# A GRU recurrence on one core: the new state from two VectorE scans, and one product group per step fewer

## The chip, the cores and the metric

The kernel runs on one core of a Trainium2 chip. The figure of merit is the device time of one execution in microseconds. A core has a matrix engine (TensorE, PE in the rows; PEld is its weight load), VectorE (DVE), ScalarE (ACT), GpSimd (POOL) and SyncE (SP, here only the queue that issues DMAs). They run side by side and wait for one another on semaphores.

## The reference

Two layers with residuals. The first is a mixture of four experts and one shared branch (each a GELU feed-forward 256 -> 1024 -> 256), which touches every row of `x` by itself. The second is a GRU over the 1024 rows of each of two sequences:

```python
def step(h, xs):
    xzt, xrt, xht = xs
    z = jax.nn.sigmoid(xzt + h @ U_z + vz)
    r = jax.nn.sigmoid(xrt + h @ U_r + vr)
    hh = jnp.tanh(xht + r * h @ U + vh)
    h_new = (1.0 - z) * h + z * hh
    return (h_new, h_new)
```

`h` has 256 features for each of 2 sequences. The 1024 steps depend on one another; the input products (`xz`, `xr`, `xh`) do not. `r * h @ U` is `(r * h) @ U`.

## The kernel before, in words

Time is cut into 8 chunks of 128 steps, a chunk into 8 bodies of 16 steps. The state lies with its features on the 128 partitions: 2 halves (`KC`) by 2 sequences (`B`), so 4 numbers per partition (`ST`). A sigmoid is written as a tanh of half its argument.

`U` in fp32 would be slow, so each of the three gate matrices is split into fp16 parts `u_high` and `u_mid`; the moving side is split too, into a HI and a LO fp16 part. The LO part is scaled up by 1024 or 2048 to stay inside fp16, and multiplies `u_low`, a third copy of `u_high` that is scaled down by the same factor. One "group" of a gate and a moving quantity is then 12 small products (`recur`, line 931): 8 with HI (`u_high`, `u_mid`; 2 output halves by 2 input halves) and 4 with LO. Each has 40 moving columns (`FILL`), of which 2 carry data and 38 are zeros. The sums collect in PSUM (`r_ps`, `z_ps`, `c_ps`) on top of the input part that `inject` (line 923) puts there once per body.

The `r` gate of the next step is not fed with the new state. The state is `h = A + Q`, with `A` the old state times (1 - z) and `Q` = z times the candidate. `A` is known before the candidate, so `old_state` (line 967) multiplies it early, and after the candidate's tanh only `Q` is multiplied. This is two groups for `r`, one for `z` (the whole new state, parts H_HI and H_LO) and one for the candidate (parts P_HI and P_LO, from `r * h`): 48 products per step.

Each engine has its own program, written out by hand. One step `t` on TensorE (`gru_body`, line 974): `r` with Q, `z` with H, window 0 of other work, candidate `c` with P, window 1 of other work, `r` of the next step with A. The other work (`gap_work`, line 944) is the feed-forward layer of the next chunk in fp32, cut into "units" (`FFN_UNITS`): every window has one unit, window 1 has two at t = 4 to 10, 12 and 14. The last body of a chunk also holds the input products of the next chunk (`gate_input`). The last chunk (steps 896 to 1023) has no feed-forward work left.

ScalarE runs the three tanhs (`gate_tanh`, line 480: r, z, c), GELUs and copies. VectorE (`gru_body`, line 687) runs 18 operations on 4 elements a step: lines 704 to 707 make P after the tanh of `r`; lines 712 to 721 make A after the tanh of `z`; lines 726 to 743 make Q, H and what the next step needs after the tanh of `c`. GpSimd splits the input parts of each body into bf16 (lines 337 to 353), scales the experts' hidden tiles (line 256) and adds the residual (`add_body`, line 355). Two bodies form one turn of a hardware loop; at the end of a turn each engine branches back.

Of the kernel before, what the change touches and what calls it, by code (L numbers as in the profile page):

```python
# [23 lines left out]
ALU = mybir.AluOpType  # L24
# [7 lines left out]
P = 128  # L32
# [3 lines left out]
LOW = 1024.0  # L36
PLOW = 2048.0
# [9 lines left out]
def moe_gru_kernel(nc, x, cond, gate_w, gate_b, time_w, time_b, ew1, eb1, ew2, eb2, sw1, sb1, sw2, sb2,  # L47
# [54 lines left out]
    with ctx:  # L102
# [29 lines left out]
        u_low = sb("u_low", [P, GATES, KC, D], F16)  # L132
# [4 lines left out]
        h_body = sb("h_body", [P, KC, SC])  # L137
# [12 lines left out]
        h_scale = sb("h_scale", [P, 1])  # L150
# [17 lines left out]
        parts = sb("parts", [P, 8, KC, FILL], F16)  # L168
        P_HI, P_LO, A_HI, A_LO, Q_HI, Q_LO, H_HI, H_LO = range(8)
        tanh_out = sb("tanh_out", [P, GATES, ST])  # L170
        st = sb("st", [P, 9, ST])
        PP, V, VV, A, AA, ZZ, QQ, HK, HH = range(9)
# [6 lines left out]
        rows_ps = xp_ps[1]  # L179
        gate_v = [g[:, 0:KC * SC].rearrange("p (m s b) -> p m s b", m=KC, b=B) for g in gate_ps]  # L180
# [63 lines left out]
        PARTS_STEP, STATE_STEP = 8, 9  # L244
# [72 lines left out]
        def _(pool):  # L317
# [37 lines left out]
            def add_body(c, j):  # L355
# [3 lines left out]
                pool.tensor_scalar(h_true[:, :, :], h_body[:, :, :], w_scale[:, :], None, ALU.mult  # L359
                                   ).then_inc(h_unscaled, 1)  # L360
                wait_apart(h_unscaled, n + 2)
# [29 lines left out]
            for g in range(GATES):  # L391
                pool.tensor_scalar(u_low[:, g, :, :], u_high[:, g, :, :],
                                   1.0 / (PLOW if g == C else LOW), None, ALU.mult).then_inc(u_split, 1)

            pool.wait_ge(scales_made, 1)
            pool.wait_ge(gate_scales_made, 2)
            split(0, 0)
            with pool.Fori(0, CH - 2) as c:
                with pool.Fori(0, BODIES - 1) as j:
                    split(c, j + 1)  # L400
                    scale_tiles(c + 1, j + 1)
                    add_body(c, j)
                scale_tiles(c + 2, 0)
                split(c + 1, 0)
                add_body(c, BODIES - 1)
            with pool.Fori(0, BODIES - 1) as j:
                split(CH - 2, j + 1)
                scale_tiles(CH - 1, j + 1)
                add_body(CH - 2, j)
            split(CH - 1, 0)  # L410
            add_body(CH - 2, BODIES - 1)
            with pool.Fori(0, BODIES - 1) as j:
                split(CH - 1, j + 1)
                add_body(CH - 1, j)
            add_body(CH - 1, BODIES - 1)


        @block.scalar
# [665 lines left out]
```

## Time and profile before

| | us |
|---|---|
| median of three runs | 2524.52 (2524.43 to 2530.35) |
| span of the profiled execution | 2531.0 |
| TensorE busy | 2338.1 (92%) |
| VectorE busy | 2022.5 (80%) |
| ScalarE busy | 755.4 (30%) |
| GpSimd busy | 337.8 (13%) |

The profiled execution's own time is its span, 2531.0 us; the profile lists nothing around it. That is 6.5 us over the median of the runs. TensorE's busy time counts a product from the moment it enters to its modelled end (about 180 ns), while the next one follows after about 25 ns, so a busy share near one does not say that the engine has no room. It is better to measure a step from the tanh rows on ScalarE: each gate has one per step, and they are never hidden by others.

### The profile page before, as it was taken

Reading aid. Unit: us, or ns where it says so; the run is one execution under the profiler, and the core shown is the slowest. Engines: PE = TensorE matmul, PEld = TensorE weight load, DVE = VectorE, ACT = ScalarE, POOL = GpSimd, SP = SyncE. Lnnn points to the kernel's source line nnn. Section 1 sums busy time; section 2 is a strip of 40 time slices with the busy share of each in tenths; the row PEclk is TensorE's granted clock in tenths of the full one; section 3 lists DMA queues with packets and bytes.
Section 4 is the critical chain, followed back from the end, with each engine's and each line's share of the span. In section 5 each row is a group of like instructions: output and inputs, shape, how many; then the busy total and the mean of one; then the engine's idle time right before and its main releaser. Section 6 shows DMA issues by size and latency. Waiting matters only on the chain.

```text
span 2531.0 us, 141144 instructions
## 1 busy us (share of the span) xinstructions
PE 2338.1 (92%) x54923; PEld 2166.7 (86%) x54923; DVE 2022.5 (80%) x18594; ACT 755.4 (30%) x3670; POOL 337.8 (13%) x623
## 2 busy tenths in 40 slices
PE   7999999999999999999999999999999898998888
PEld 5798898888988899888998889888898898977777
DVE  5288887888878888788878888788888887888888
ACT  2332233332332333322333233332233232232222
POOL 3011111111111111111111111111111111100000
PEclk8999999999999999999999999999999999998899
DMA  4411111111111111111111111111111111000000
GB/s 144 124 47 38 44 39 34 45 35 38 44 35 38 45 37 40 37 38 38 44 37 36 44 37 42 40 35 38 44 40 33 45 37 36 24 5 5 4 5 5
DMA packets 143677, 99.88 MB, mean 39 GB/s; under 512 B 13664, under 2 KB 142999, under 8 KB 143004
## 3 DMA queue, kind: packets, MB, share of 16 engines
q1 hardware_dynamic: 141840, 90.49, 12.5%
q8 instruction: 465, 7.62, 1.3%
q14 instruction: 208, 1.70, 0.2%
q10 hardware_dynamic: 1164, 0.07, 0.0%
HBM read 88.41 MB, written 2.10 MB: 36 GB/s over the span
## 4 chain that ended last, share of the span: by engine, by line
PE 73%; DVE 18%; issue 6%; ACT 2%; DMA 0%; DVEq 0%; SPq 0%; POOL 0%; POOLq 0%; ACTq 0%
PE r_ps L936 25%; PE up_ps L878 13%; PE c_ps L936 12%; PE y_ps L896 12%; PE z_ps L936 8%; DVE parts L704 2%; DVE parts L707 2%; ACT tanh_out L482 2%; PE xp_ps L910 2%; DVE st L714 1%; DVE st L743 1%; DVE parts L729 1%; DVE st L705 1%; DVE st L712 1%; DVE parts L741 1%
## 5 line engine op out<-in xcount | busy, mean ns | idle before, releaser
L936 PE MATMUL r_ps<-parts,u_high 128*128 128x40 f16 x8192 | 671.9, 182 | 108.4 <-issue 90.2
L936 PE MATMUL r_ps<-parts,u_mid 128*128 128x40 f16 x8192 | 664.0, 180 | 0.0
L936 PEld LDWEIGHTS r_ps<-parts,u_high 128*128 128x128 f16 x8192 | 543.4, 97 | 140.1 <-issue 91.8
L878 PE MATMUL up_ps<-feat,up_w 128*128 (+2 forms) x2380 | 542.1, 322 | 0.0
L936 PE MATMUL r_ps<-parts,u_low 128*128 128x40 f16 x8192 | 536.6, 182 | 3.5 <-DVE parts L729 2.3
L936 PEld LDWEIGHTS r_ps<-parts,u_mid 128*128 128x128 f16 x8192 | 516.3, 97 | 13.0 <-issue 1.1
L896 PE MATMUL y_ps<-hidden,down_w 128*128 128x128 f32 (+1 forms) x2380 | 496.9, 314 | 8.3 <-DVE hidden L256 8.3
L704 DVE SCALAR_TENSOR_TENSOR parts<-tanh_out,st 128x4 f16<-128x4 f32 x1024 | 197.4, 193 | 322.7 <-ACT tanh_out L482 258.9
L482 ACT ACTIVATE tanh_out<-r_ps 128x4 f32<-128x4 f32 x1024 | 177.2, 173 | 870.1 <-PE r_ps L936 870.1
L936 PE MATMUL c_ps<-parts,u_high 128*128 128x40 f16 x4096 | 349.9, 183 | 33.8 <-DVE parts L704 12.5
L878 PEld LDWEIGHTS up_ps<-feat,up_w 128*128 128x128 f32 x2380 | 367.4, 196 | 9.5 <-issue 3.0
L896 PEld LDWEIGHTS y_ps<-hidden,down_w 128*128 128x128 f32 x2380 | 345.9, 192 | 19.4 <-DVE hidden L256 12.2
L482 ACT ACTIVATE tanh_out<-c_ps 128x4 f32<-128x4 f32 x1024 | 177.5, 173 | 611.7 <-PE c_ps L936 611.7
L936 PEld LDWEIGHTS r_ps<-parts,u_low 128*128 128x128 f16 x8192 | 350.1, 97 | 10.2 <-DVE parts L729 3.6
L936 PEld LDWEIGHTS c_ps<-parts,u_high 128*128 128x128 f16 x4096 | 263.2, 97 | 109.5 <-DVE parts L704 53.8
L936 PE MATMUL z_ps<-parts,u_high 128*128 128x40 f16 x4096 | 343.1, 181 | 0.0
L936 PE MATMUL z_ps<-parts,u_mid 128*128 128x40 f16 x4096 | 342.2, 181 | 0.0
L936 PE MATMUL c_ps<-parts,u_mid 128*128 128x40 f16 x4096 | 340.8, 180 | 0.0
L936 PE MATMUL c_ps<-parts,u_low 128*128 128x40 f16 x4096 | 272.0, 182 | 9.5 <-DVE parts L707 6.9
L936 PE MATMUL z_ps<-parts,u_low 128*128 128x40 f16 x4096 | 268.8, 182 | 10.9 <-DVE parts L741 10.5
L936 PEld LDWEIGHTS c_ps<-parts,u_mid 128*128 128x128 f16 x4096 | 259.5, 97 | 7.4
L936 PEld LDWEIGHTS z_ps<-parts,u_mid 128*128 128x128 f16 x4096 | 257.7, 97 | 0.0
(137 smaller groups left out, 4577.5 us busy)
## 6 DMA issues: line engine op xcount, KB each, us to landing
up_w<-in_L_cond_ew SPq DMA_DIRECT2D x256, 128.0 KB, 2.4
down_w<-in_L_cond_ew SPq DMA_DIRECT2D x256, 128.0 KB, 2.1
up_w<-in_L_cond_sw SPq DMA_DIRECT2D x64, 128.0 KB, 3.0
down_w<-in_L_cond_sw SPq DMA_DIRECT2D x64, 128.0 KB, 2.2
x_rows<-in_x SPq DMA_DIRECT2D x8, 256.0 KB, 4.9
out<-out_rows SPq DMA_DIRECT2D x128, 16.0 KB, 1.8
cf<-in_L_cond_C_r SPq DMA_DIRECT2D x1, 256.0 KB, 5.8
cf<-in_L_cond_C_z SPq DMA_DIRECT2D x1, 256.0 KB, 6.0
```

The costliest lines, as they stand in the source:

```text
L482: act.activation(tanh_out[:, g, :].rearrange("p (m b) -> p m b", b=B), gate_v[g][:, :, t, :], ACT.Tanh, scale=1.0 if g == C else 0.5).then ...
L704: dve.scalar_tensor_tensor(p(P_HI), tr, 1.0, s(HH), ALU.add, ALU.mult).then_inc(part_ready, 1)
L705: dve.scalar_tensor_tensor(s(PP), tr, 1.0, s(HK), ALU.add, ALU.mult).then_inc(state, 1)
L707: dve.scalar_tensor_tensor(p(P_LO), p(P_HI), -PLOW, s(PP), ALU.mult, ALU.add).then_inc(part_ready, 1)
L712: dve.scalar_tensor_tensor(s(VV), tz, 1.0, s(HK), ALU.add, ALU.mult).then_inc(state, 1)
L714: dve.tensor_scalar(s(ZZ), tz, 1.0, half_s[:, :], ALU.add, ALU.mult).then_inc(state, 1)
L729: dve.scalar_tensor_tensor(p(Q_LO), p(Q_HI), -LOW, s(QQ), ALU.mult, ALU.add).then_inc(part_ready, 1)
L741: dve.scalar_tensor_tensor(p(H_LO), p(H_HI), -LOW, s(HK), ALU.mult, ALU.add).then_inc(part_ready, 1)
L878: last = mm(up_ps[e % 2][:, at:at + width], up_w[:, e, k, :], cols[k, half], start=(k == 0 and at == 0), stop=(k == KC - 1), skip_group_ch ...
L896: last = mm(y_ps[:, m * COLS + at:m * COLS + at + width], down_w[:, e, m * P:(m + 1) * P], hidden[:, e % 2, at:at + width], start=False, s ...
L910: last = mm(xp_ps[g % 2][:, m * COLS:(m + 1) * COLS], wx[:, g, k, m * P:(m + 1) * P], cols[k, None], start=(m == 0 and k == 0), stop=(k == ...
L936: last = mm(gate_ps[g][:, m * SC + t * B:m * SC + t * B + FILL], w[:, g, k, m * P:(m + 1) * P], parts[:, part, k, :], start=False, stop=st ...
```

## The change

* The `r` gate is fed with the whole new state. `old_state` and its 12 products per step are gone; `r` and `z` take the same moving parts (`h_parts`), so 36 products per step are left.
* The state is kept in units scaled by `GAIN` (the weights' scale has another exponent, the tanh takes `scale=0.5 / GAIN`, the input parts are scaled up, GpSimd scales the state down again). The LO part needs no scaling of its own then: it is the plain difference, and it multiplies `u_high`. `u_low` is gone.
* The new state comes from `tensor_tensor_scan`, a running `state = cand * state + blend` over 8 elements per partition, in pairs: the even element of `cand` is 0 and of `blend` is z, which sets the state to z; the odd one of `cand` is the candidate's tanh and of `blend` the kept part of the old state, which gives the new state. It is run twice on the same operands, once to fp16 (`h_parts` HI) and once to fp32 (`h_hist`). A subtraction makes LO, another small operation the `-h/2` of the next step. VectorE has 9 operations a step in place of 18.
* The moving operand of `r` and `z` is now read with a stride: 20 groups of 16 bytes, two fp16 numbers 4 bytes apart in each. That of the candidate stays contiguous.
* `h_hist` holds 32 steps; GpSimd unscales it with two operations per body in place of one (`add_body`), and its loops are written out by pairs of bodies.

```diff
-            def recur(g, t, part, weights, stop=False):
+            def recur(g, t, part, i, weights, stop=False):
                 for m in range(KC):
                     for k in range(KC):
-                        for i, w in enumerate(weights):
+                        moving = (p_parts[:, i, k, :] if part is p_parts else
+                                  h_parts[:, i, :, (2 * k) * B + 1:(2 * k + 2) * B:2])
+                        for at, w in enumerate(weights):
...
-                    pe.wait_ge(part_ready, before_n + (Q_HI + 1))
-                    recur(R, t, Q_HI, BOTH)
-                    pe.wait_ge(part_ready, before_n + (Q_LO + 1))
-                    recur(R, t, Q_LO, DOWNED, stop=True).then_inc(preact, 1)
+                    pe.wait_ge(part_ready, before_n + 3)
+                    recur(R, t, h_parts, HI, BOTH)
+                    pe.wait_ge(part_ready, before_n + 4)
+                    recur(R, t, h_parts, LO, HIGH, stop=True).then_inc(preact, 1)
...
-                    if t < STEPS - 1:
-                        old_state(t + 1, before_n + PARTS_STEP)
-                    elif not last:
+                    if t == STEPS - 1 and not last:
                         pe.wait_ge(split_ready, n + 3)
                         inject(R, False)
-                        old_state(0, before_n + PARTS_STEP)
```

```diff
                     dve.wait_ge(act_done, gate0 + 2)
...
+                    dve.tensor_scalar(blend_v[:, :, 0], tz, 1.0, half_s[:, :], ALU.add, ALU.mult).then_inc(state, 1)
+                    dve.scalar_tensor_tensor(blend_v[:, :, 1], tz, 1.0, st[:, HH, :], ALU.subtract, ALU.mult
+                                             ).then_inc(state, 1)
                     dve.wait_ge(act_done, gate0 + 3)
-                    dve.tensor_tensor(p(Q_HI), s(ZZ), tc, ALU.mult).then_inc(part_ready, 1)
-                    dve.scalar_tensor_tensor(s(QQ), tc, LOW, s(ZZ), ALU.mult, ALU.mult).then_inc(state, 1)
-                    dve.wait_ge(state, s0 + 7)
-                    dve.scalar_tensor_tensor(p(Q_LO), p(Q_HI), -LOW, s(QQ), ALU.mult, ALU.add
-                                             ).then_inc(part_ready, 1)
...
+                    dve.wait_ge(state, s0 + 3)
+                    if t == 0:
+                        dve.wait_ge(h_unscaled, KC * (n + 1))
+                    dve.tensor_tensor_scan(h_parts[:, HI, 0, :], cand[:, :], blend[:, :], 0.0, ALU.mult, ALU.add
+                                           ).then_inc(part_ready, 1)
+                    dve.tensor_tensor_scan(h_hist[:, first + t, :], cand[:, :], blend[:, :], 0.0, ALU.mult, ALU.add
+                                           ).then_inc(state, 1)
+                    dve.wait_ge(state, s0 + 4)
+                    dve.tensor_tensor(h_parts[:, LO, 0, :], h_hist[:, first + t, :], h_parts[:, HI, 0, :],
+                                      ALU.subtract).then_inc(part_ready, 1)
+                    dve.tensor_scalar(st[:, HH, :], h_now[:, first + t, :], -0.5, None, ALU.mult).then_inc(state, 1)
```

Two places of the programs show what stands in a row. First TensorE, from the candidate's LO products to the first products with the new state, in a step whose window 1 has one unit (`up_ps`). Before:

```order
L936 MATMUL c_ps<-parts,u_low 128x40 x4
L878 MATMUL up_ps<-feat,up_w 128x128
L936 MATMUL r_ps<-parts,u_high 128x40
L936 MATMUL r_ps<-parts,u_mid 128x40
L936 MATMUL r_ps<-parts,u_high 128x40
L936 MATMUL r_ps<-parts,u_mid 128x40
L936 MATMUL r_ps<-parts,u_high 128x40
L936 MATMUL r_ps<-parts,u_mid 128x40
L936 MATMUL r_ps<-parts,u_high 128x40
L936 MATMUL r_ps<-parts,u_mid 128x40
L936 MATMUL r_ps<-parts,u_low 128x40 x4
L936 MATMUL r_ps<-parts,u_high 128x40
```

These twelve products are those of A; the last row is the first product with Q. Of the change, at the same place:

```order
L929 MATMUL c_ps<-p_parts,u_high 128x40 x4
L869 MATMUL up_ps<-feat,up_w 128x128
L929 MATMUL r_ps<-h_parts,u_high 128x40
L929 MATMUL r_ps<-h_parts,u_mid 128x40
L929 MATMUL r_ps<-h_parts,u_high 128x40
L929 MATMUL r_ps<-h_parts,u_mid 128x40
L929 MATMUL r_ps<-h_parts,u_high 128x40
L929 MATMUL r_ps<-h_parts,u_mid 128x40
L929 MATMUL r_ps<-h_parts,u_high 128x40
L929 MATMUL r_ps<-h_parts,u_mid 128x40
L929 MATMUL r_ps<-h_parts,u_high 128x40 x4
```

The first `r` product after the unit now waits for the new state itself. Second VectorE, from the candidate's tanh (the wait on `act_done`) to the end of the step; the wait on `state` is for the result of an operation just before. Before:

```order
L726 TENSOR_TENSOR parts<-st,tanh_out 128x2x2 [waits act_done]
L727 SCALAR_TENSOR_TENSOR st<-tanh_out,st 128x4
L729 SCALAR_TENSOR_TENSOR parts<-parts,st 128x2x2 [waits state]
L731 SCALAR_TENSOR_TENSOR parts<-st 128x2x2
L733 TENSOR_TENSOR st<-st 128x4
L735 SCALAR_TENSOR_TENSOR h_body<-st 128x2x2
L741 SCALAR_TENSOR_TENSOR parts<-parts,st 128x2x2 [waits state]
L743 TENSOR_SCALAR st<-st 128x4
```

Of the change, with the two operations after the tanh of `z` ahead of it:

```order
L720 TENSOR_SCALAR blend<-tanh_out,half_s 128x4 [waits act_done]
L721 SCALAR_TENSOR_TENSOR blend<-tanh_out,st 128x4
L728 SCALAR_TENSOR_TENSOR h_parts<-cand,blend 128x8 [waits state,act_done]
L730 SCALAR_TENSOR_TENSOR h_hist<-cand,blend 128x8
L733 TENSOR_TENSOR h_parts<-h_hist,h_parts 128x8 [waits state]
L735 TENSOR_SCALAR st<-h_hist 128x4
```

The scans stand as `SCALAR_TENSOR_TENSOR` rows (L728, L730) on 8 elements. The HI part is again the first operation after the tanh, the LO part again the third, with the same wait for the second.

## Rows read from the trace of the kernel before

**Rows 1.** The page, first line: the span.
```profile
span 2531.0 us, 141144 instructions
```

**Rows 2.** Timeline, last chunk, one undisturbed half step: start us, us, engine, line, operation.
```profile
2334.94 0.17 ACT L482 ACTIVATE tanh_out<-c_ps 128x4 f32<-128x4 f32 x1 [0.49 <-PE c_ps L936]
...
2335.14 0.16 DVE L726 TENSOR_TENSOR parts<-st,tanh_out 128x4 f16<-128x4 f32 x1
...
2335.22 0.16 DVE L727 SCALAR_TENSOR_TENSOR st<-tanh_out,st 128x4 f32<-128x4 f32 x1
...
2335.37 0.19 PE L936 MATMUL r_ps<-parts,u_high 128*128 128x40 f16 x1
...
2335.41 0.16 DVE L729 SCALAR_TENSOR_TENSOR parts<-parts,st 128x4 f16<-128x4 f16 x1
...
2335.64 0.27 PE L936 MATMUL r_ps<-parts,u_low 128*128 128x40 f16 x4
...
2335.94 0.17 ACT L482 ACTIVATE tanh_out<-r_ps 128x4 f32<-128x4 f32 x1 [0.83 <-PE r_ps L936]
```

**Rows 3.** Timeline of ACT, a body with feed-forward: steps with two units, then one.
```profile
786.71 0.17 ACT L482 ACTIVATE tanh_out<-r_ps 128x4 f32<-128x4 f32 x1 [0.59 <-PE r_ps L936]
...
787.72 0.17 ACT L482 ACTIVATE tanh_out<-c_ps 128x4 f32<-128x4 f32 x1 [0.54 <-PE c_ps L936]
788.85 0.17 ACT L482 ACTIVATE tanh_out<-r_ps 128x4 f32<-128x4 f32 x1 [0.96 <-PE r_ps L936]
...
798.83 0.17 ACT L482 ACTIVATE tanh_out<-c_ps 128x4 f32<-128x4 f32 x1 [0.53 <-PE c_ps L936]
799.84 0.17 ACT L482 ACTIVATE tanh_out<-r_ps 128x4 f32<-128x4 f32 x1 [0.83 <-PE r_ps L936]
```

**Rows 4.** Chain that ended last, in time, in the first of those steps.
```profile
788.22 0.59 PE r_ps L936 x24
```

**Rows 5.** Timeline of ACT, last body of a chunk (with input products).
```profile
1012.20 0.17 ACT L482 ACTIVATE tanh_out<-c_ps 128x4 f32<-128x4 f32 x1 [0.87 <-PE c_ps L936]
...
1013.77 0.17 ACT L482 ACTIVATE tanh_out<-r_ps 128x4 f32<-128x4 f32 x1 [0.77 <-PE r_ps L936]
```

**Rows 6.** Timeline around a turn of the loop, PE and then ACT.
```profile
811.95 0.19 PE L936 MATMUL r_ps<-parts,u_high 128*128 128x40 f16 x1 [4.25 <-issue]
```
```profile
814.27 0.17 ACT L482 ACTIVATE tanh_out<-c_ps 128x4 f32<-128x4 f32 x1 [0.83 <-PE c_ps L936]
...
815.74 0.17 ACT L482 ACTIVATE tanh_out<-r_ps 128x4 f32<-128x4 f32 x1 [0.89 <-PE r_ps L936]
```

**Rows 7.** Windows: busy by engine, then granted clock (PEclk), DMA share, GB/s.
```profile
1344.00:1648.00 304.00, 286.21 (x6921) 269.06 (x6918) 247.49 (x2309) 93.12 (x453) 42.51 (x80) 0.96 0.14 39
...
2247.00:2524.00 277.00, 238.70 (x6200) 208.74 (x6196) 235.06 (x2288) 69.06 (x390) 18.66 (x44) 0.88 0.02 5
```

**Rows 8.** Windows, then ACT's timeline: a step at the low clock.
```profile
2357.50:2359.60 2.10, 1.94 (x53) 1.71 (x51) 1.83 (x18) 0.51 (x3) 0.00 (x0) 0.50 0.00 0
```
```profile
2357.49 0.17 ACT L482 ACTIVATE tanh_out<-r_ps 128x4 f32<-128x4 f32 x1 [1.05 <-PE r_ps L936]
...
2358.54 0.17 ACT L482 ACTIVATE tanh_out<-c_ps 128x4 f32<-128x4 f32 x1 [0.47 <-PE c_ps L936]
2359.62 0.17 ACT L482 ACTIVATE tanh_out<-r_ps 128x4 f32<-128x4 f32 x1 [0.91 <-PE r_ps L936]
```

**Rows 9.** Groups of DVE instructions: busy us, mean ns, idle before.
```profile
L714 DVE TENSOR_SCALAR st<-tanh_out,half_s 128x4 f32<-128x4 f32 x1024 | 235.8, 230 | 0.0
...
L727 DVE SCALAR_TENSOR_TENSOR st<-tanh_out,st 128x4 f32<-128x4 f32 x1024 | 159.5, 156 | 0.0
...
L256 DVE TENSOR_TENSOR hidden<-hidden,expert_w 128x128 f32<-128x128 f32 x36 | 14.8, 430 | 47.9 <-ACT hidden L477 47.9
```

**Rows 10.** Timeline, second step of an odd body: DVE, then POOL.
```profile
774.70 0.56 DVE L741 SCALAR_TENSOR_TENSOR parts<-parts,st 128x4 f16<-128x4 f16 x1
...
775.88 0.52 DVE L707 SCALAR_TENSOR_TENSOR parts<-parts,st 128x4 f16<-128x4 f16 x1
```
```profile
774.70 0.55 POOL L347 TENSOR_TENSOR xrest<-xpart,xsplit 128x192 f32<-128x192 bf16 x1 [0.19 <-POOL xsplit L345]
```

More of the change, by code:

```diff
@@ L35 @@
 STEPS = 16
-LOW = 1024.0
-PLOW = 2048.0
+GAIN = 2.0 ** 12
 FP16_MAX = 65504.0
@@ L165, in moe_gru_kernel @@
         spread = sb("spread", [B, BR, B])
[L168 to L172, printed above, removed]
+        p_parts = sb("p_parts", [P, 2, KC, FILL], F16)
+        h_parts = sb("h_parts", [P, 2, FILL // B, 2 * ST], F16)
+        HI, LO = range(2)
+        tanh_out = sb("tanh_out", [P, 2, ST])
+        cand = sb("cand", [P, 2 * ST])
+        blend = sb("blend", [P, 2 * ST])
+        st = sb("st", [P, 2, ST])
+        body_mark = sb("body_mark", [P, 1])
+        PP, HH = range(2)
         gate_ps = [pb("r_ps"), pb("z_ps"), pb("c_ps")]
@@ L179, in moe_gru_kernel @@
         rows_ps = xp_ps[1]
+        h_now = h_hist[:, :, :].rearrange("p s (e two) -> p s e two", two=2)[:, :, :, 1]
+        c_now = cand[:, :].rearrange("p (e two) -> p e two", two=2)[:, :, 1]
+        blend_v = blend[:, :].rearrange("p (e two) -> p e two", two=2)
+        gain = lambda g: 2.0 * GAIN if g == C else GAIN
         gate_v = [g[:, 0:KC * SC].rearrange("p (m s b) -> p m s b", m=KC, b=B) for g in gate_ps]
@@ L397, in _, with body, bodies @@
             split(0, 0)
+            def body(c, j, first, ffn):
+                split(c, j + 1)
+                if ffn:
+                    scale_tiles(c + 1, j + 1)
+                add_body(c, j, first)
+            def bodies(c, ffn):
+                with pool.Fori(0, BODIES - 2, 2) as j:
+                    body(c, j, 0, ffn)
+                    body(c, j + 1, STEPS, ffn)
+                body(c, BODIES - 2, 0, ffn)
             with pool.Fori(0, CH - 2) as c:
[L399 to L402, printed above, removed]
+                bodies(c, True)
                 scale_tiles(c + 2, 0)
                 split(c + 1, 0)
[L405 to L409, printed above, removed]
-            split(CH - 1, 0)
[L411 to L415, printed above, removed]
+                add_body(c, BODIES - 1, STEPS)
+            bodies(CH - 2, True)
+            split(CH - 1, 0)
+            add_body(CH - 2, BODIES - 1, STEPS)
+            bodies(CH - 1, False)
+            add_body(CH - 1, BODIES - 1, STEPS)
         @block.scalar
@@ L702, in gru_body @@
+                    prev = sq(h_now[:, (first + t - 1) % ROUND, :])
+                    p = lambda i: p_parts[:, i, :, 0:B]
                     dve.wait_ge(act_done, gate0 + 1)
[L703 to L705 removed]
+                    dve.wait_ge(state, s0 - 1)
+                    dve.scalar_tensor_tensor(p(HI), tr, 1.0, prev, ALU.add, ALU.mult).then_inc(part_ready, 1)
@@ L965, in gap_work @@
                         gate_input(tail, tail_cols, *product)
-            def old_state(t, count):
-                pe.wait_ge(part_ready, count + (A_HI + 1))
-                recur(R, t, A_HI, BOTH)
-                pe.wait_ge(part_ready, count + (A_LO + 1))
-                recur(R, t, A_LO, DOWNED)
             def gru_body(c, j, first, cols, ffn=None, tail=None, tail_cols=None, last=False):
```

114 lines of the change are left out of this document (42 added, 72 removed).

## The prediction

> **What bounds the kernel now.** I read the page first, for the span of 2531.0 us [rows 1]; the median of the runs is 6.5 us below it, so a sum made against the span is lowered by 6.5 at the end. The shares of busy time say little: TensorE's counts each short product at its full latency. I then measured the steps on ScalarE, from one tanh to the next. A step has two halves: from the tanh of r to the tanh of c (R to C), and from there to the tanh of r of the next step (C to R).
>
> In the last chunk nothing else runs on TensorE, and C to R is 2335.94 - 2334.94 = 1.00 us [rows 2]. Where it goes: tanh to first VectorE operation 0.20; its successor 0.08 later; the third, which waits for the second, 0.19 later; from there to the four LO products 0.23; from these to the next tanh 0.30. The eight HI products start at 2335.37 and need about 0.2, so they are through just before the LO part is there. The half step is thus a chain of latencies, and it ends on the LO part, not on TensorE's work. R to C is 1.01 in a step with a unit in its window (786.71 to 787.72) [rows 3], again the chain: tanh, P_HI, the fp32 product, P_LO, products. A C to R with one unit is 1.01 as well (798.83 to 799.84), so one unit plus the twelve old products fit under the chain. Only with two units is it longer, 1.13 (787.72 to 788.85) [rows 3]: there TensorE is the bound. In the last body of a chunk, with the input products, it is 1.57 [rows 5]; TensorE is the bound by far. After each turn of the loop TensorE issues nothing for some 4 us [rows 6], the clock falls, and the step after it has a C to R of 1.47 where a step in the last chunk at the low clock takes 1.08 [rows 6, 8]. So the kernel is a latency chain of some 2.0 us a step, with places where TensorE sticks out over it. That decides what twelve products fewer are worth: nothing where the chain ends last.
>
> **The change part by part.**
>
> *Twelve products per step less.* Twenty-four products take 0.59 [rows 4], so twelve 0.30. In a two-unit window 1.13 - 0.30 = 0.83 would be left for TensorE, below the chain; what is late next is the chain at 1.00, and the gain is 0.13. By the table of units there are 9 such windows in each of 49 bodies (7 in each of 7 chunks), and 2 more in each of the 6 last bodies that have two units without being bound by input products: 453 x 0.13 = 59 us. In those 6 last bodies, seven windows each are long by input products, 1.57 would become 1.27, still over the chain: 42 x 0.30 = 13 us. After the 26 turns of the loop, 1.47 falls towards 1.08; I take 0.35: 9 us. The old products also stood ahead of the branch itself, so the pause begins earlier: 26 x 0.30 = 8 us. In all other windows, seven per body and nearly the whole last chunk, they were hidden and give nothing. Sum: 89 us less.
>
> *VectorE's path to the new state.* Q_HI, QQ, Q_LO are replaced by scan, scan, subtraction: same place, same number, same wait. Let x be what the three cost more on the chain. The trace has no scan. Bounds: not below 0, since 4 elements more cannot be quicker; at the top each scan is as dear as the dearest 4-element row, 230 against 156 ns [rows 9], two of them 0.15. The nearest row is the ordinary operation: 128 elements take 430 and 4 take 156 ns, which is 2.2 ns an element, so 4 elements more cost 9 ns at most. I take x = 0.025, three operations at some 8 ns. It counts in every C to R that the chain ends, about 956 of 1024: 24 us more. Both ends are kept: 0 and 143 us.
>
> The Trainium skill ("DVE: opcode table, instruction layouts, handler registers and perf-mode slots", section "6. Datapath and trigger behaviour") says that this scan runs at half throughput, because its result is routed back to an earlier stage. Taken as an estimate from that page, 8 elements at two cycles of 0.96 GHz are about 8 ns more per scan than I allow, x would be 0.04, and the sum 15 us higher. No row here can tell.
>
> *The nine other VectorE operations that go* (A_HI, A, A_LO, H_LO and so on) lay beside TensorE's work or after the LO part; they give nothing directly. The z gate no longer waits for H_LO, which is off the chain too. The first scan waits for two semaphores; so did line 704 before, at the same distance from its tanh.
>
> *The strided moving operand.* No row has a product like it. At least it costs nothing. At most each product with `h_parts` feeds at half the rate: by the low clock, where the columns come at half the rate, C to R is 0.08 longer with twelve more products in it and R to C 0.04 [rows 8], so up to 0.04 on the chain, 38 us. I take 0, since at the full clock 40 columns leave room under the 25 ns between products. On this the Trainium skill ("Advanced Engine Details and Errata", section "SBUF Cachelines") says that two hits on a line of 16 bytes are needed to hide the memory's latency. The stride here has exactly two per line, so that page gives no cost either.
>
> *The clock.* With 48 products a step the granted clock over the last chunk was 0.88 [rows 7]: TensorE fell to 1.2 GHz in part of it, though nothing paused but the turns. 36 products in the same time are less, so I take it to stay at 1.2 GHz for all of that chunk. The price is from rows: R to C 1.05, C to R 1.08 against 1.01 and 1.00, of which some was the old products; 0.10 a step on about 96 steps: 10 us more. In the other chunks the clock was 0.96 [rows 7], low only after turns and in the last bodies; a step there keeps its 36 products and two to three fp32 units, more than the last chunk had in all, so I leave it at 2.4 GHz.
>
> *Set-up and GpSimd.* `u_low` is made while the feed-forward of chunk 0 runs; two small VectorE operations come in the same place; nothing on the end. GpSimd has one more operation per body, in `add_body`, which is waited for only a step and a half later; 0.
>
> Sum: -89 + 24 + 10 = -55. 2531.0 - 55 = 2476; less the 6.5, 2469.5 us.
>
> **The rivals.**
>
> *The scans are dear: slower.* The place is C to R, in every step. The gains and the clock's 10 leave 79 us, so it decides at x = 79 / 956 = 0.083. At the top end, 0.15, the time is 2531 - 79 + 143 - 6.5 = 2588; half way, 0.115, it is 2555. For it: nothing in the trace is a scan, and one VectorE form of 4 elements does take 230 ns. Against it: it is issued as the ordinary three-operand form.
>
> *VectorE was crowded more than I count: faster still.* An operation of VectorE lasts until GpSimd's ends when they meet: 0.56 and 0.52 in place of 0.16 [rows 10], and with 18 operations in a row the next ones are pushed back. With nine there is slack. If that frees some 0.9 per body over 56 bodies, 50 us: 2420. Against it: the operations on the chain, P_HI and P_LO among them, meet GpSimd just as before.
>
> *The strided operand is slow:* 38 us more on the chain, 2507.
>
> *TensorE's clock falls in the feed-forward chunks too.* Then every step there is bound by TensorE at 1.2 GHz; going by C to R 1.47 and more [rows 6], at least 0.2 a step, 180 us: 2640. The load there speaks against it.
>
> **How the numbers follow.** Forecast (x from 0 to 0.06): 0.69. Crowding freed: 0.12. Strided operand or x from 0.06 to 0.083: 0.09, of which 0.04 within 0.3% and the rest faster. Scans dear: 0.08. Clock: 0.02. Within 0.3%, 7.6 us, is what a measurement here cannot tell from no change. Faster 0.69 + 0.12 + 0.05 = 0.86, same 0.04, slower 0.10. The likeliest alone runs from x = 0 (2445) to x = 0.06 (2503). The range goes down to 2425 for part of the crowding and up to 2510 for the stride.
>
> **What would show it.** C to R in two-unit windows falls from 1.13 to 1.03, and so does every C to R of the full clock, one-unit windows rising from 1.01 to 1.03. R to C stays at 1.01. Scan rows last about 165 to 175 ns, the second starts 0.08 to 0.09 after the first. The last bodies of a chunk show C to R of 1.27. The last chunk has a clock near 0.5 and steps of 2.13. The pauses at the turns stay near 4 us. I am wrong if C to R is over 1.08 everywhere, if the clock is low outside the last chunk, or if the gain sits in R to C.

## The result: slower, by a term that was taken as zero

The changed kernel takes 2619.4 us (median of 4 runs, 2613.2 to 2623.1), the kernel before 2527.4 us (4 runs, 2524.4 to 2530.4). The ratio is 1.0366, 95% interval 1.0349 to 1.0383. The forecast of 2469.5 us is 150 us too low, its range ends at 2510, and the sign is wrong. The profiled execution has a span of 2611.4 us against 2531.0 [rows 1], and the granted clock over the whole of it is 0.894 against 0.952.

The page of the changed kernel: the span, busy time by engine, the granted clock in 40 slices, and from the costliest groups one of TensorE and the first scan (columns: busy us, mean ns of one, idle before and its releaser).

```profile
span 2611.4 us, 108361 instructions
...
PE 2307.6 (88%) x42635; PEld 2081.1 (80%) x42635; DVE 1322.1 (51%) x9448; ACT 758.1 (29%) x3670; POOL 346.4 (13%) x684
...
PEclk8998998999988999899998999989999999965555
...
L929 PE MATMUL r_ps<-h_parts,u_high 128*128 128x40 f16 x8192 | 654.2, 209 | 275.7 <-DVE h_parts L728 130.6
...
L728 DVE TENSOR_TENSOR_SCAN h_parts<-cand,blend 128x8 f16<-128x8 f32 x1024 | 179.7, 175 | 359.2 <-ACT cand L491 358.6
```

The scan lasts 175 ns, as forecast. The line above it holds the surprise, though one has to know what to look for: a product of the r gate lasts 209 ns, while before each group of these short products had a mean of 180 to 183.

Timeline of the changed kernel over one step with a unit in the first window and two in the second; it answers to [rows 2] and [rows 3].

```profile
820.19 0.17 ACT L491 ACTIVATE tanh_out<-r_ps 128x4 f32<-128x4 f32 x1 [0.93 <-PE r_ps L929]
...
820.40 0.16 DVE L714 SCALAR_TENSOR_TENSOR p_parts<-tanh_out,h_hist 128x4 f16<-128x4 f32 x1 [0.57 <-ACT tanh_out L491]
...
820.45 0.47 PE L869 MATMUL up_ps<-feat,up_w 128*128 x2
...
820.75 0.18 PE L929 MATMUL c_ps<-p_parts,u_high 128*128 128x40 f16 x1
...
821.25 0.17 ACT L491 ACTIVATE cand<-c_ps 128x4 f32<-128x4 f32 x1 [0.42 <-PE c_ps L929]
...
821.45 0.17 DVE L728 TENSOR_TENSOR_SCAN h_parts<-cand,blend 128x8 f16<-128x8 f32 x1 [0.29 <-ACT cand L491]
821.54 0.16 DVE L730 TENSOR_TENSOR_SCAN h_hist<-cand,blend 128x8 f32<-128x8 f32 x1
821.69 0.20 PE L929 MATMUL r_ps<-h_parts,u_high 128*128 128x40 f16 x1
...
821.74 0.17 DVE L733 TENSOR_TENSOR h_parts<-h_hist,h_parts 128x8 f16<-128x8 f32 x1
...
821.99 0.33 PE L929 MATMUL r_ps<-h_parts,u_high 128*128 128x40 f16 x4
...
822.35 0.17 ACT L491 ACTIVATE tanh_out<-r_ps 128x4 f32<-128x4 f32 x1 [0.46 <-PE r_ps L929]
```

C to R is 1.10 us (821.25 to 822.35). Piece by piece against [rows 2]: tanh to first scan 0.20 (0.20); to the second 0.09 (0.08); to the subtraction 0.20 (0.19); to the four LO products 0.25 (0.23); from these to the next tanh 0.36 (0.30). VectorE's part costs 0.02, just what was forecast. The rest, 0.08, lies behind VectorE. The two-unit windows did fall from 1.13, but to 1.10 and not to 1.03. The others rose from 1.00: to 1.10 for most one-unit windows, to 1.19 at steps 3 and 13 of a body (counted from 0, and the two-unit window of step 7 is as long), and to 1.12 in the last chunk. R to C, which no part of the change was thought to touch, is 1.06 (820.19 to 821.25): the twelve z products end late, the unit behind them too, and the first c product starts 0.35 after P_HI.

Weight loads in the same step show the pace, first of products with `h_parts`, then with `p_parts` (columns: start, length).

```profile
820.06 0.11 PEld L929 LDWEIGHTS z_ps<-h_parts,u_mid 128*128 128x128 f16 x1
820.10 0.11 PEld L929 LDWEIGHTS z_ps<-h_parts,u_high 128*128 128x128 f16 x1
820.14 0.11 PEld L929 LDWEIGHTS z_ps<-h_parts,u_mid 128*128 128x128 f16 x1
...
820.81 0.10 PEld L929 LDWEIGHTS c_ps<-p_parts,u_mid 128*128 128x128 f16 x1
820.83 0.10 PEld L929 LDWEIGHTS c_ps<-p_parts,u_high 128*128 128x128 f16 x1
820.86 0.10 PEld L929 LDWEIGHTS c_ps<-p_parts,u_mid 128*128 128x128 f16 x1
```

With the strided operand they start 0.04 us apart, with the contiguous one 0.025; the medians over the whole trace are 39 and 25 ns. Both have 40 columns. A set of twelve takes 0.47 us instead of 0.30.

A turn of the loop in the changed kernel, PE's timeline; it answers to [rows 6].

```profile
831.90 0.20 PE L929 MATMUL r_ps<-h_parts,u_high 128*128 128x40 f16 x1 [3.85 <-issue]
...
834.81 0.25 PE L929 MATMUL r_ps<-h_parts,u_high 128*128 128x40 f16 x2 [2.37 <-issue]
```

There are two pauses now, at each of the 17 turns of chunks 0 to 5. C to R over such a turn is 7.0 to 8.2 us, where it was 4.9 to 5.8. The four turns of chunks 6 and 7, whose loops are other copies of the code, keep one pause and take 4.5 to 5.0 (5.1 to 6.4 before).

Where the 80 us of span went, summed from the starts of the tanh rows (us; C = C to R, R = R to C; bodies 0 to 6 of chunks 0 to 6 from the fourth step on; the last two columns are experiments below):

| stretch | before | after | 24 columns | 24 columns, shifted |
|---|---|---|---|---|
| until the recurrence starts | 129.7 | 122.4 | 122.7 | 122.4 |
| C, 441 two-unit windows | 499.4 | 493.6 | 455.2 | 455.0 |
| C, other windows | 185.7 | 209.2 | 186.6 | 186.5 |
| R | 683.5 | 680.1 | 674.0 | 673.8 |
| first three steps of these bodies | 363.1 | 386.0 | 356.0 | 355.7 |
| C over the 19 turns | 104.4 | 136.8 | 139.5 | 89.1 |
| last bodies of these chunks | 281.4 | 285.2 | 265.6 | 268.9 |
| last chunk | 277.4 | 291.6 | 278.5 | 278.3 |
| behind the recurrence | 6.3 | 6.5 | 6.5 | 6.5 |
| span | 2531.0 | 2611.4 | 2484.7 | 2436.1 |

The first line is not the change's: the recurrence starts at 121.7 to 124.2 us in some profiled executions and at 128.3 to 129.7 in others, kernels of both families among either. What sets it stays open, and differences of less than 7 us between spans are not read. Of what rose, the turns are the largest line (32 us); the two lines that rose without a turn, the other C windows and the first three steps, make 46, and the last chunk 14.

### The profile page after: what moved, and what is told of

Read it like the earlier page. It is cut to its first block and busy times, and to the rows that moved or that the text cites. A ratio compares the mean times of both kernels' runs of the same rounds, so it can differ in the third digit from the quotient of the medians.

```text
span 2611.4 us, 108361 instructions
## 1 busy us (share of the span) xinstructions
PE 2307.6 (88%) x42635; PEld 2081.1 (80%) x42635; DVE 1322.1 (51%) x9448; ACT 758.1 (29%) x3670; POOL 346.4 (13%) x684
## 5 line engine op out<-in xcount | busy, mean ns | idle before, releaser
L929 PE MATMUL r_ps<-h_parts,u_high 128*128 128x40 f16 x8192 | 654.2, 209 | 275.7 <-DVE h_parts L728 130.6
L929 PEld LDWEIGHTS r_ps<-h_parts,u_high 128*128 128x128 f16 x8192 | 514.9, 106 | 432.0 <-issue 197.2
L929 PE MATMUL z_ps<-h_parts,u_high 128*128 128x40 f16 x8192 | 653.0, 210 | 0.0
L929 PEld LDWEIGHTS z_ps<-h_parts,u_high 128*128 128x128 f16 x8192 | 550.4, 110 | 0.0
L929 PE MATMUL c_ps<-p_parts,u_high 128*128 128x40 f16 x8192 | 501.0, 184 | 6.3 <-DVE p_parts L714 3.8
L929 PEld LDWEIGHTS c_ps<-p_parts,u_high 128*128 128x128 f16 x8192 | 442.3, 99 | 33.6 <-DVE p_parts L714 11.3
L929 PE MATMUL z_ps<-h_parts,u_mid 128*128 128x40 f16 x4096 | 452.0, 210 | 0.0
L929 PE MATMUL r_ps<-h_parts,u_mid 128*128 128x40 f16 x4096 | 443.9, 208 | 0.0
L728 DVE TENSOR_TENSOR_SCAN h_parts<-cand,blend 128x8 f16<-128x8 f32 x1024 | 179.7, 175 | 359.2 <-ACT cand L491 358.6
L929 PE MATMUL c_ps<-p_parts,u_mid 128*128 128x40 f16 x4096 | 350.3, 183 | 0.0
L929 PEld LDWEIGHTS z_ps<-h_parts,u_mid 128*128 128x128 f16 x4096 | 350.3, 110 | 0.0
```

What stands on the lines that cost most here:

```text
L728: dve.tensor_tensor_scan(h_parts[:, HI, 0, :], cand[:, :], blend[:, :], 0.0, ALU.mult, ALU.add).then_inc(part_ready, 1)
L929: last = mm(gate_ps[g][:, m * SC + t * B:m * SC + t * B + FILL], w[:, g, k, m * P:(m + 1) * P], moving, start=False, stop=stop and k == KC ...
```

## The experiments

**The strided operand made shorter.** The r and z products stream 24 of their 40 columns, in the same layout, so the stride stays and 12 groups of 16 bytes are read in place of 20; the c products keep 40.

```
+HFILL = 24
...
+                        width = FILL if part is p_parts else HFILL
                         moving = (p_parts[:, i, k, :] if part is p_parts else
-                                  h_parts[:, i, :, (2 * k) * B + 1:(2 * k + 2) * B:2])
+                                  h_parts[:, i, 0:HFILL // B, (2 * k) * B + 1:(2 * k + 2) * B:2])
```

> The changed kernel with one edit: the products of r and z stream 24 columns in place of 40 (22 of zeros in place of 38); those of the candidate keep 40. Theory: the strided moving operand is the cost, at about 1 ns a column (39 ns from product to product with 40 columns, where the contiguous ones are 25 ns apart). With 24 columns the products of h_parts come 25 ns apart, C to R falls from 1.10 to 1.02-1.03 and R to C from 1.057 to 1.01, 0.12 us in each of 896 steps: 2619 - 110 = about 2505 us, so faster than before too. Rival: the two scans and the subtraction are the cost of C to R; then nothing but the spacing changes, C to R stays over 1.08 and the time over 2590. A second rival: with fewer columns TensorE's clock falls to 1.2 GHz in the feed-forward chunks, and the time goes over 2650.

Measured: 2486.8 us (2485.2 to 2489.4), ratio to the kernel before 0.9848 (0.9832 to 0.9865), so 133 us less than the changed kernel. Timeline of a half step of this kernel:

```profile
1113.42 0.17 ACT L492 ACTIVATE cand<-c_ps 128x4 f32<-128x4 f32 x1 [0.54 <-PE c_ps L931]
1113.62 0.17 DVE L729 TENSOR_TENSOR_SCAN h_parts<-cand,blend 128x8 f16<-128x8 f32 x1 [0.37 <-ACT cand L492]
...
1113.71 0.16 DVE L731 TENSOR_TENSOR_SCAN h_hist<-cand,blend 128x8 f32<-128x8 f32 x1
...
1113.91 0.17 DVE L734 TENSOR_TENSOR h_parts<-h_hist,h_parts 128x8 f16<-128x8 f32 x1
...
1114.13 0.27 PE L931 MATMUL r_ps<-h_parts,u_high 128*128 128x24 f16 x4
...
1114.44 0.17 ACT L492 ACTIVATE tanh_out<-r_ps 128x4 f32<-128x4 f32 x1 [0.43 <-PE r_ps L931]
```

C to R is 1.02, in two-unit and one-unit windows alike (median 1.025 in both), which is the forecast of the prediction; in the windows of the last bodies with input products it is 1.27, as forecast, where the changed kernel has 1.43. The products lie 25 ns apart, LO to tanh is 0.31 again. The scans are the same in both kernels, so they are not what made the change slow. This run alone does not tell the layout from the number of columns; the next one does, and contiguous products of 30 and 40 columns both come 25 ns apart at 2.4 GHz (the run with 30 columns, below).

**The stride alone, put into the kernel before.** No scan, no other change; `parts` of A, Q and H in groups of 16 bytes as in the changed kernel.

```
-        parts = sb("parts", [P, 8, KC, FILL], F16)
+        parts = sb("parts", [P, 8, FILL // B, 2 * ST], F16)
+        p_parts = sb("p_parts", [P, 2, KC, FILL], F16)
```

> The kernel before with one edit: the moving parts of r and z (A, Q and H) lie as in the change, two numbers 4 bytes apart in each group of 16 bytes; no scan, still 48 products, u_low kept. Theory: the stride alone costs. Products of r and z 39 ns apart, C to R of the last chunk 1.10, two-unit windows bound by TensorE at 1.13 + 24 x 0.014 = 1.47, R to C 1.06: about 4.9 us a body over 56 bodies and some 20 us in the last chunk, 2527 + 290 = 2820 us. Rival: the stride costs nothing by itself and the scans do; then 2527 us, unchanged.

Measured: 2845.0 us, ratio 1.1264 (1.1245 to 1.1283). Products 39 ns apart, two-unit C to R 1.47, one-unit 1.25 to 1.34, last chunk 1.28, R to C 1.07. The stride slows the old program too, and by more, since it has 36 such products a step instead of 24.

**What of the stride it is.** The kernel before with three layouts at once, 40 columns each: A one column per 16 bytes, Q an adjacent pair per 16 bytes, H every second element without gaps.

```
+        a_parts = sb("a_parts", [P, 2, KC, 8 * FILL], F16)
+        q_parts = sb("q_parts", [P, 2, FILL // B, 8], F16)
+        z_parts = sb("z_parts", [P, 2, KC, 2 * FILL], F16)
```

> The kernel before, with the moving columns of its three sets of state products in three layouts, 40 columns each, values unchanged: the set issued early (A) has one column every 16 bytes, the one behind the r gate's tanh chain (Q) has adjacent pairs, one pair per 16 bytes, the z set (H) every second element without gaps. Theory of lines: a product pays about 1.95 ns for each 16 bytes that it touches, so 78 ns apart for A, 39 for Q, 25 (the floor seen for contiguous ones; 10 lines make 19.5) for H. Rival, by column: any strided operand pays about 1 ns a column, 39 ns for A and H and 25 or 39 for Q. Time by the theory of lines: Q adds 12 x 14 ns on the chain of 896 + 128 steps, about 170 us, and A up to 12 x 53 ns = 0.64 us a step where nothing hides it: 2700 to 3300 us.

Weight loads of this kernel, one stretch:

```profile
1394.35 0.12 PEld L949 LDWEIGHTS r_ps<-a_parts,u_mid 128*128 128x128 f16 x1
1394.42 0.12 PEld L949 LDWEIGHTS r_ps<-a_parts,u_high 128*128 128x128 f16 x1
1394.49 0.12 PEld L949 LDWEIGHTS r_ps<-a_parts,u_mid 128*128 128x128 f16 x1
...
1395.01 0.11 PEld L949 LDWEIGHTS r_ps<-q_parts,u_mid 128*128 128x128 f16 x1
1395.05 0.11 PEld L949 LDWEIGHTS r_ps<-q_parts,u_high 128*128 128x128 f16 x1
1395.09 0.11 PEld L949 LDWEIGHTS r_ps<-q_parts,u_mid 128*128 128x128 f16 x1
...
1395.49 0.10 PEld L949 LDWEIGHTS z_ps<-z_parts,u_high 128*128 128x128 f16 x1
1395.52 0.10 PEld L949 LDWEIGHTS z_ps<-z_parts,u_mid 128*128 128x128 f16 x1
1395.54 0.10 PEld L949 LDWEIGHTS z_ps<-z_parts,u_high 128*128 128x128 f16 x1
```

Medians at 2.4 GHz: 73 ns for A, 39 for Q, 25 for H; 3174.7 us in all (one run). H is strided and costs nothing, Q has its pairs side by side and costs 39. So a stride as such is not what is paid for; the pace follows the number of 16-byte groups that the operand touches: 40 of them take 73 ns, 20 take 39, ten are hidden under the 25 ns that any product takes here, and so are the twelve of the 24-column kernel. That is 1.8 to 1.95 ns a group. The size of the group is not shown by itself: A, Q and H reach over 640, 320 and 160 bytes, and a price of 0.11 to 0.12 ns for each byte reached over, or one by groups of 32 bytes, fits these medians as well. A price by groups of 8 bytes does not, since H touches 20 of them, as Q does.

**Is it the clock?** The last chunk runs at 1.2 GHz in the changed kernel. To see what that is worth, the kernel before with 30 columns everywhere:

```
-FILL = 40
+FILL = 30
```

> The kernel before with one edit: 30 moving columns in every short product in place of 40, so as many columns a step as the change streams (48 x 30 = 36 x 40 = 1440). Theory: in the last chunk TensorE stays at 1.2 GHz (granted clock near 0.5 in place of 0.88), a step there goes from 2.0-2.1 to 2.12, and the other chunks keep their clock: 10 to 12 us more, about 2538. Rival: the clock of the last chunk depends on something else (how long products run, or waits), it stays at 0.88 and the time at 2527.

Measured: 2526.2 us, ratio 0.9997 (0.9982 to 1.0013). Window of its last chunk, then two tanh rows of it:

```profile
2240.00:2510.00 270.00, 232.63 (x5989) 205.80 (x5989) 227.63 (x2210) 67.02 (x377) 18.68 (x44) 0.50 0.02 5
```
```profile
2326.60 0.17 ACT L482 ACTIVATE tanh_out<-c_ps 128x4 f32<-128x4 f32 x1 [0.51 <-PE c_ps L936]
2327.62 0.17 ACT L482 ACTIVATE tanh_out<-r_ps 128x4 f32<-128x4 f32 x1 [0.85 <-PE r_ps L936]
```

The chunk runs at 1.2 GHz throughout, as expected, and takes 279.3 us against 277.4, half a step 1.02 against the 1.05 and 1.08 of [rows 8]. At 1.2 GHz products of 40 contiguous columns start 33 ns apart and those of 30 start 27 ns apart (not 25, as the expectation of the run with 30 c columns has it). So with nothing but the chain, as in the last chunk, the low clock costs little, and most of what it does cost is the width of the zeros. The 10 to 12 us that were expected did not come.

**The second pause at the turns.** The changed kernel, and then the 24-column kernel, with 40 small products ahead of TensorE's program, which do nothing but shift its code by 80 instructions.

```
             pe.wait_ge(ident_made, 3)
+            for _ in range(40):
+                mm(up_ps[0][:, 0:32], ident16[:, :], ident16[:, 0:32], start=True, stop=True, skip_group_check=True)
```

> The changed kernel with 40 small products added once at TensorE's start (under 3 us, while it waits for data), so that all of its later instructions lie 80 further on. In the changed kernel TensorE pauses twice after each turn of the loop of chunks 0 to 5: 3.85 us, then some 20 instructions, then 2.37 us; before there was one pause of 4.25. Theory: the second pause is the fetch of the next block of instructions, and comes because the branch target lies just ahead of the end of a block. Shifted by 80 it lies elsewhere, the second pause goes at 18 turns, and with it some microseconds of low clock: 2619 - 45 = 2575 us. Rival: the pause belongs to the changed loop itself (its waits, or the smaller program), and the time stays within 8 us of 2619.

> The 24-column kernel (2486.8 us) with 40 small products ahead of the recurrence, which shift TensorE's code by 80 instructions. Theory: the second pause behind each loop turn comes from where the loop body lies in the code, so the 21 turns of 7.1 to 7.9 us fall to about 4.8 us, with less low clock behind them: about 2435 us. Rival: the position that suited the changed kernel does not suit this one, turns stay at 7.6 us and the time at 2487 us.

Measured: 2577.3 us (2574.7 to 2579.0) for the first, 42 less than the changed kernel; 2436.3 us (2433.8 to 2437.9), ratio 0.9636 (0.9613 to 0.9659), for the second, 50 less than its own. PE at a turn of the second:

```profile
1068.52 0.18 PE L933 MATMUL r_ps<-h_parts,u_high 128*128 128x24 f16 x1 [4.22 <-issue]
```

One pause of 4.2 us is left, as in [rows 6], and C over the 19 turns falls from 139.5 to 89.1 us. This is all of the gain: the other lines of the table hardly move.

What TensorE waits for in these pauses can be read from the packets of the queue that the page calls `instruction`. The pages of the changed kernel and of the shifted one:

```profile
q8 instruction: 384, 6.29, 1.0%
```
```profile
q8 instruction: 369, 6.05, 1.0%
```

Packets, MB and share: 15 packets of 16 KB fewer with the shift (384 and 369 for the 24-column pair too). By the packets' times in these four traces, the first pause ends 1.5 to 1.9 us after such a packet has landed, at all 21 turns of each. Where there is a second pause, a further packet starts within 0.6 us of the last product before it, and TensorE goes on 1.2 to 1.6 us after that one has landed; with the shift a packet comes at the same time, and TensorE does not stop for it. Between the two pauses lie 10 products with their weight loads, every time. So by these times the pauses are waits for code, as the expectation has it, and the second one comes where the code at the loop's start runs out after ten products. That a boundary between blocks lies just there is argued from one shift, not shown. The kernel before with the same shift:

> The kernel before with 40 small products ahead of the recurrence, code shifted by 80 instructions as in the two shifted runs. Theory: the pause behind a loop turn depends on where the loop lies in the code and not on the change, so here too it can move either way: turns of 5.0 to 5.7 us become 7 to 8 us (2570 us) or 4.4 (2505 us). Rival: the second pause belongs to the changed kernel's shorter loop, and the kernel before stays within 3 us of its 2526 us with turns of 5.0 to 5.7 us.

Measured: 2530.6 us (2526.0 to 2534.8), ratio 1.0014 (1.0001 to 1.0027), turns of 4.9 to 6.0 us. By this the rival holds as far as one shift can tell: the old loop, with 48 products a step, shows one pause in both positions (and 465 instruction packets in both), the new one shows one or two. Two positions are too few to say that the old loop never has a second pause.

**Register waits ahead of the r products.** In the changed kernel some windows, those of steps 3, 7 and 13, are longer than the rest:

```profile
866.90 0.17 ACT L491 ACTIVATE cand<-c_ps 128x4 f32<-128x4 f32 x1 [0.42 <-PE c_ps L929]
...
867.10 0.17 DVE L728 TENSOR_TENSOR_SCAN h_parts<-cand,blend 128x8 f16<-128x8 f32 x1 [0.30 <-ACT cand L491]
...
867.39 0.10 PEld L929 LDWEIGHTS r_ps<-h_parts,u_high 128*128 128x128 f16 x1 [0.41 <-issue]
```

The first r product follows the scan by 0.32 us (its PE row is at 867.42) where 0.24 is usual; C to R is 1.19. TensorE's waits for the next unit's weights stand directly ahead of these products, where the old-state products stood before. Moved behind the z products, in the 24-column kernel, without and with the shift, and then in the changed kernel:

```
-                    for kind, e, unit in FFN_UNITS.get((t + window, 1 - window), ()):
+                    for kind, e, unit in FFN_UNITS[t, 1] if window == 0 else ():
...
                     recur(Z, t, h_parts, LO, HIGH, stop=True).then_inc(preact, 1)
+                    for kind, e, unit in FFN_UNITS[t, 0] if ffn and t > 0 else ():
+                        if unit == 0:
+                            (up_ready if kind == UP else down_ready)(*ffn, e)
```

> The 24-column kernel (2486.8 us), with the register waits for the next expert unit's weights and inputs issued by TensorE after the z products of the next step instead of directly ahead of its r products. Theory: in some windows the first r product starts 0.32 us or more after the scan instead of 0.24, and C to R is 1.18 to 1.25 instead of 1.00, because a register wait stands directly in front of the r products; moved, these windows (about four per body, some 0.2 us each, 56 bodies) fall to 1.00 to 1.03 us and the kernel to about 2442 us. Rival: the waits cost the same wherever they stand, R to C rises by what C to R loses, and the time stays at 2487 us.

> Both edits of the two runs beside it: the register waits behind the z products and the 40 small products. If they are independent, the gains add: about 2395 us, C to R 1.00 to 1.03 us in nearly all windows and turns of 4.8 us. If the longer steps were only slack that the clock gives back (more products per microsecond, less low clock), it would be lower by a further 10 us; if one takes away what the other gains, 2435 us.

> The changed kernel (2619.4 us) with the register waits for the next unit's weights and inputs behind the z products instead of directly ahead of the r products. Theory: with 39 ns products TensorE reaches these waits so late that they are not covered; at steps 3, 7, 13 and 0 of a body C to R is 1.19 us instead of 1.10 and TensorE stands 0.41 us in issue ahead of the first r product. Moved, these windows fall to 1.10 us: four or five per body x 56 bodies x 0.09 = 20 to 23 us, so about 2598 us; with 24 columns the same edit was worth nothing because the wait is covered there. Rival: the 0.09 us has another cause in those windows, and the time stays within 3 us of 2619.

Measured: 2490.5, 2439.9 and 2614.3 us, against 2486.8, 2436.3 and 2619.4 without the edit. The first expectation rested on a misreading: in the 24-column kernel C to R is 1.02 to 1.04 in all these windows already, and the 1.18 to 1.25 that I had put there are R to C at steps 3, 5 and 8, as long before the change. TensorE comes to the waits early enough there. Its 4 us more lie in two turns of the last chunk, which went from 4.5 and 4.8 to 7.3 and 7.5, a second pause again. In the changed kernel the windows do what the theory says, 1.19 to 1.10, and C outside the first three steps loses 13 us; yet the median falls by 5 only. In the profiled execution the recurrence starts 5.9 us later, and the last chunk is 5.6 longer, since two of its turns went from 4.5 and 5.0 to 7.7 and 7.8: moved code, again. So this cost is real, about 17 us of the changed kernel with the first steps counted, of which R to C takes 3 back, and the second-order result of the stride.

**Width of the c products.** On the best kernel so far, c with 30 columns; then 56 while expert work runs and 30 elsewhere.

```
+CFILL = 30
...
+                        width = CFILL if part is p_parts else HFILL
```

> The shifted 24-column kernel (2436.3 us) with the c products at 30 columns instead of 40. Theory: at the low clock 40 columns lie 33 ns apart and 30 columns 25, so each of its low-clock half steps on the p_parts path gains 12 x 8 ns less what is hidden: some 0.02 us in the last chunk's 128 steps and some of the 43 us of low clock per chunk, about 2431 us in all. Rival: less work per microsecond lets the clock stay low for longer behind the turns (43 us per chunk becomes 55 or more), and the time rises to 2445 us or more.

> The shifted 24-column kernel (2436.3 us), c products with 56 columns while the expert work runs and 30 columns in the last chunk and the body ahead of it without expert work. With 40 columns the clock was low for 42 us of a middle chunk, with 30 for 54 us. Theory: wider c products keep the clock up sooner, low clock falls to some 30 us per chunk; each such us costs about 0.25 us, so 7 x 12 x 0.25 = 21 us, with 2 us from the last chunk: about 2415 us; at the full clock 56 columns still lie 25 ns apart. Rival: at 1.2 GHz 56 columns lie 47 ns apart, and in the low stretches that remain the c products cost 12 x 14 ns = 0.17 us a step more; if the low clock does not shorten, some 20 low steps a chunk x 7 make it 24 us worse, 2460 us.

Measured: 2453.7 us (2450.8 to 2455.2) and 2454.0 us (2449.4 to 2458.4), both worse than the 2436.3 with 40. Clock over the whole run 0.859 with 30 columns, 0.879 with 40, 0.886 with 56: in these three runs the mean clock rose with the width, as the first rival and the second theory had it. But 30 columns lose 8 us in two-unit windows, and 56 lose 5 us in R to C and 9 in the first steps, some of which run at 1.2 GHz, where products of 56 columns start 46 to 47 ns apart. Each of the two profiled executions also had the late start, 7 us of its span. The part of the 17 us in either median that this explains can't be told apart from the widths.

## Why the prediction was wrong

**The step that failed** is "The strided moving operand": "I take 0, since at the full clock 40 columns leave room under the 25 ns between products". The runs show 39 ns in place of 25, 24 times a step. With 24 columns, which bring these products back to 25 ns, the kernel gains 133 us, with everything else in place. Its upper end failed as well, 0.04 on the chain and 38 us, for two reasons. It was read off the low clock, where 40 contiguous columns lie 33 ns apart, so it bounded columns at half rate and not the groups that the layout touches, which are slower still, at either clock. And it counted one place. The price comes in at least three: C to R in every window (0.07 to 0.08), R to C by the z products ahead of the unit and of c (0.05), and the register waits that now lie bare (0.09 in some windows). A resource with no row before needed a bound of its own, and the pace of contiguous columns at the low clock was no such bound.

The Trainium skill's rule ("Advanced Engine Details and Errata", section "SBUF Cachelines") asks for at least two hits on each 16-byte line to hide the memory's latency, and the prediction read two as enough. For TensorE's moving operand this case's runs do not agree with that: two columns a line gave 39 ns, with the pair adjacent or not; four a line gave 25.

**Removed products: right.** The two-unit windows were to fall from 1.13 to the chain plus x. With 24 columns they are 1.025, and the 441 windows give 44 us; forecast were 57 of the 59 for these, less 11 for x, 46. The windows with input products in the last bodies fell by 0.30 to 1.27, and those bodies by 16 us in all (13 forecast). In the changed kernel itself the 441 two-unit windows gained 6 us only: they end on the chain as forecast, but on a chain whose r products are slow, at 1.10. Of the two terms at the turns, the earlier start of the pause was sized too small: with one pause left the 19 turns take 15 us less than before, 0.8 each and not 0.30. The 9 us for the half step behind a turn did not come at all: it is 1.52 with 24 columns where it was 1.47.

**Scans: right.** x was taken as 0.025; C to R with 24 columns is 1.025 where it was 1.003 in the one-unit windows. The rival of dear scans is refuted, 175 ns and a second scan 0.09 behind the first. Slower came true through another mechanism.

**The pauses: wrong.** "The pauses at the turns stay near 4 us" holds for the first of two. The second cost 42 us in the changed kernel. Nothing in the trace of before told of it, but the pause itself was there [rows 6], and a change that alters TensorE's code on both sides of a branch makes its length an unknown, which deserved a range. The count was off too: 26 turns were assumed, and 21 show a pause, 19 of them ahead of the last chunk.

**The clock: place right, size too large.** The last chunk is at 1.2 GHz throughout:

```profile
2310.00:2604.00 294.00, 223.77 (x4717) 189.66 (x4718) 157.57 (x1164) 69.81 (x393) 20.95 (x53) 0.50 0.01 4
```

I priced it at 10 us from a step that also had the old products in it; the 24-column kernel, with the same clock and the scans, takes 278.5 against 277.4. In the other chunks the clock is lower than I said, with 25 to 39 us of 1.2 GHz per chunk instead of 17 to 24, and 40 to 55 with 24 columns, mostly behind the turns. The rival that the clock falls in these chunks too came true for some steps of them: a step at 1.2 GHz with a unit in each window has an R to C of 1.34 with 24 columns, where the same step at 2.4 GHz has 1.00, so there the low clock is dear. By its own numbers that rival stood at 2469.5 + 180, about 2650, and not at 2640.

**Crowded VectorE: partly right.** The place was right: steps 2 and 3 of odd bodies outside the last take 107.0 us in sum before (21 bodies), 92.1 with 24 columns. That is 15 us, not 50, since it does not happen in even bodies; there the same two steps rose from 120.9 to 131.6 us, since some of them now run at 1.2 GHz. A second place was not named: at step 10 (counted from 0) of all 49 bodies, GpSimd's scaling of a hidden tile held up the last VectorE operation before the tanh of r,

```profile
795.20 0.59 DVE L743 TENSOR_SCALAR st<-st 128x4 f32<-128x4 f32 x1
```
```profile
795.12 0.64 POOL L256 TENSOR_TENSOR hidden<-hidden,expert_w 128x256 f32<-128x256 f32 x1 [3.62 <-ACT hidden L477]
```

and P_HI with it. Its R to C fell from 1.26 to 1.06, 10 us in all, since VectorE is done before GpSimd starts. So the rival is right for about half of its 50 us.

Put together, 24 columns and a position of the code without the second pause, which is luck, give 2436 us. That is below the forecast, but the 24-column kernel without that luck, 2487, is above it. So fewer products and the scan gain by themselves, and the layout that the scan writes makes the change lose.

## What to carry to other kernels

For short products, count the 16-byte groups that the moving operand touches, padding included: twelve were hidden here and twenty set the pace, not the columns (between the two nothing was measured). When an edit changes an operand's layout and the trace has no such row, treat its price as open, multiply it by every product that uses it, and look for every queue behind those products; then measure the layout by itself first. And if a loop's turn is a visible cost, shift the code once before judging a change of a few per cent.

## What the runs showed of the hardware

- A TensorE product of 40 fp16 columns starts 25 ns after the one before with 4 or 8 columns per 16 bytes, 39 ns with 2, 73 ns with 1. The 39 and 73 ns are the same at both levels of the clock: in the changed kernel's last chunk the products lie as far apart as at 2.4 GHz.
- At 1.2 GHz products of 56 contiguous columns start 46 to 47 ns apart, of 40 33 ns and of 30 27 ns, and those of the 24-column kernel's r and z gates 27 ns as well; at 2.4 GHz 30 and 40 give 25 and 56 give 26.
- Behind a turn of the loop TensorE starts no product for 3.9 to 5.4 us, and in some positions of the code pauses again, 2.3 to 3.3 us from start to start, after ten products. Each pause ends 1.2 to 2.2 us after a 16 KB packet of the queue `instruction` has landed. A shift by 80 instructions took the second pause away (42 and 50 us), and an edit elsewhere in the loop brought one into the last chunk.
- A scan of 8 elements lasts 175 ns, and the operation behind it starts after 90 ns, where 4-element operations of two tensors last 156 and follow after 80.
